# A Mamba and attention kernel on one core: mask weights on VectorE, the turned u copied by ScalarE, a first turn that waits for its own loads, 15 images a block

## The chip, the cores and the metric

The kernel runs on one core of one Trainium2 chip. The metric is the device time of one execution in microseconds; three executions of the kernel before took 8346.27 to 8347.81 us, median 8347.58. Engine names: PE is TensorE, DVE VectorE, ACT ScalarE, POOL GpSimd, SP SyncE, which issues the transfers.

## The reference, cut to what matters

For each of 32 images (128 channels, 32 by 32 pixels, so 1024 tokens) three layers follow each other. In short:

```python
# layer 0: attention over the 1024 tokens of the image
attn = softmax(Q.T @ K * scale); t = V @ attn.T + x
# layer 1: h = LN(t) through Mamba, both directions, then layer norm and a small MLP
xc, z = split(x @ in_proj); xc = silu(conv4(xc)); dt, Bm, Cm = xc @ x_proj
h[t] = exp(dt * A) * h[t-1] + dt * Bm * xc;  y = (h * Cm).sum + xc * Dp;  y = y * silu(z)
m = fwd(y) @ out_proj + bwd(y) @ out_proj;   t2 = m + mlp(LN(m))
# layer 2: the heaviest 511 of 1024 tokens get a feed-forward, scaled by their weight
weights = x @ wr;  keep = top_k(weights)[:511];  x[keep] += gelu(x[keep] @ w1) @ w2 * weights[keep]
```

The Mamba state has 16 components for each of 256 inner channels, in two directions; the work with it is the bulk of the kernel. (Each layer adds its input to its output and the input of a layer is normed where the layer asks for it.)

## The kernel before, in words

An image's Mamba layer is 64 **steps**: four quarters (two directions, two halves of 512 tokens), each with 16 state components. At step n, with two halves of 128 channels each,

- ACT (lines 848 and 860) makes `da` = exp(dt A) and half of `ub` = u times B for step n + 2,
- POOL (L1042) makes the other half of `ub` for step n + 2, and then (L1056) `g` = h times C of step n, 128 by 1024,
- PE turns `ub` of step n + 1 into PSUM (L518) and adds the turned `g` of step n - 1 to y (L522),
- DVE scans (L1160): `h` of step n from `da` and the turned `ub`,
- SP loads the row of C for step n + 4 into a ring of four tiles `c_all` (L461), once `g` has freed the tile.

Everything else is laid beside these steps. Each step has four **slots** (4n to 4n + 3), and the tables `AT_...` and `LN_...` say in which slot an engine does which piece: on DVE scan, slots 4n and 4n+1, second scan, slots 4n+2 and 4n+3; on PE and ACT in the same way; on POOL `ub`, two slots, `g`, two slots; on SP four slots, then the load of C. An engine takes its instructions in this order and waits at each for its semaphores, so a slot is a place in a queue, not a time. In slots of the same 64 steps run

- the preparation of the next quarter k + 1 (projection, convolution, silu, dt, u): among it DTMAX and U on DVE, DTKEEP on ACT (L919), UT on PE, which turns u into PSUM, and UKEEP, the copy of the turned u to `u_tok` (L1248, DVE). `u_tok` is what both makers of `ub` read, from the quarter's first step on, two steps ahead;
- the closing of quarter k (turn y, skip, gate, project);
- the attention of the next image, through the PSUM banks X: eight blocks of scores, maximum, exponential, turn, product (AT_S to AT_T1);
- the MLP and the feed-forward of the image before: MT adds the Mamba sum to `t1_old` on POOL (L1074), T1OLD moves `t1` to `t1_old` by a transfer (L472) after both MT sums; later LN, W (the router's weights), RANK on DVE (a comparison with all 1024 weights for each block), WK, which makes the mask `is_kept` (L1286), WTIMES, `w_kept` = mask times weight on POOL (L1108), HID, GELU and FFN, T3 on DVE (L1293), OUT on PE, OUTKEEP on ACT (L950) and STORE (L475), the transfer of the result, which waits for OUTKEEP.

The images are run in **blocks** (`turns`): a first turn with the attention of image 0 alone, image 0, a loop over images 1 to 30 with `JOINED` = 5 images in each block, image 31, and a last turn that finishes it. Each block ends in a barrier of all engines, and the semaphores are cleared. Inside a block an image follows the last without one. Before all this the setup block loads 38 weights on SP (L303); DVE and ACT wait for all of them, and DVE multiplies the convolution's weights together (L334). The first turn then loads x of image 0 (L480), and PE waits for it (L730).

Of the kernel before, what the change touches and what calls it, by code (L numbers as in the profile page):

```python
# [5 lines left out]
def conv_attn_mamba_mod_kernel(nc, I, out):  # L6
# [10 lines left out]
    P = 128  # L17
# [28 lines left out]
    JOINED = 5  # L46
# [4 lines left out]
    AT_YT = (4, 68, 132, 198)  # L51
    AT_SKIP = (8, 74, 137, 202)
    AT_GATE = ((6, 6), (84, 88), (136, 154), (203, 208))
    AT_CONV = ((8, 8, 8, 9), (75, 76, 79, 81), (135, 136, 137, 152), (204, 205, 205, 205))
    AT_PROJ = (17, 74, 140, 203)
    AT_PROJKEEP = (21, 80, 143, 203)
    AT_TAPS = ((25, 26, 27), (84, 87, 87), (148, 156, 158), (208, 209, 209))
    AT_XC = (24, 86, 156, 210)
    AT_Z = ((27, 27), (86, 86), (156, 157), (157, 157))
    AT_ZKEEP = (24, 86, 157, 157)  # L60
    AT_ROWS = ((28, 28), (88, 91), (158, 163), (211, 211))
    AT_ROWKEEP = (28, 95, 164, 213)
    AT_M = ((13, 13), (92, 95), (164, 164), (212, 212))
    AT_MKEEP = (19, 98, 168, 216)
    AT_B = (32, 97, 168, 215)
    AT_BKEEP = (37, 103, 172, 218)
    AT_DT = (35, 101, 170, 215)
    AT_DTCUT = (39, 106, 175, 219)
    AT_DTEXP = (38, 106, 174, 217)
    AT_DTLN = (38, 112, 177, 217)  # L70
# [8 lines left out]
    AT_XTOK = 13  # L79
    AT_Q = (11, 12)  # L80
    AT_QKEEP = 12
    AT_K = (19, 20)
    AT_KKEEP = 23
    AT_V = (24, 27)
    AT_VKEEP = 32
    AT_S = (36, 37, 48, 48, 60, 61, 81, 81, 109, 109, 118, 118, 132, 134, 154, 154)
    AT_MAX = (43, 52, 66, 87, 114, 122, 139, 163)
    AT_EXP = (39, 52, 65, 90, 113, 122, 139, 168)
    AT_PT = (43, 52, 67, 96, 114, 124, 144, 173)
    AT_PTKEEP = (42, 55, 67, 97, 115, 123, 145, 174)  # L90
    AT_RINV = (47, 55, 74, 110, 118, 133, 148, 178)
    AT_PV = (46, 47, 55, 56, 68, 70, 106, 107, 116, 116, 127, 131, 148, 148, 178, 179)
    AT_T1 = (50, 61, 83, 110, 120, 133, 153, 182)

    LN_STATS = {0: (131, 194), 1: (15, 30), 2: (211, 213)}
    LN_AGGR = {0: (154, 195), 1: (16, 44), 2: (212, 213)}
    LN_POW = {0: 192, 1: 48, 2: 211}
    LN_APPLY = {0: (197, 197), 1: (58, 67), 2: (216, 216)}
    LN_TURN = {0: 199, 1: 182, 2: 217}
    LN_KEEP = {0: 201, 1: 180, 2: 217}  # L100

    AT_MT = (24, 30)
    AT_B2 = (29, 68)
    AT_T1OLD = 38
    AT_W1 = (184, 185, 189, 189)
    AT_HID1 = (184, 190)
    AT_LEAKY = (191, 195)
    AT_W2 = (195, 195, 195, 195)
    AT_T2 = 199
    AT_BASE = (221, 222)  # L110
    AT_W = (222, 222)
    AT_WKEEP = 221
    AT_WTURN = 225
    AT_WCOL = 229
    AT_EARLIER = 223
    AT_RANK = (230, 231, 231, 232, 234, 234, 234, 239)
    AT_WK = 240
    AT_WTIMES = 237
    AT_HID = (226, 226, 229, 229, 231, 231, 232, 232)
    AT_GELU = (227, 227, 228, 228)  # L120
    AT_FFN = (233, 233, 233, 234, 239, 239, 240, 242)
    AT_T3 = (243, 247)
    AT_OUT = 246
    AT_OUTKEEP = 248
    AT_STORE = 244
# [9 lines left out]
    FIRST_T1 = tuple(FIRST + 6 + 4 * i for i in range(8))  # L135

# [5 lines left out]
    with ctx:  # L142
# [127 lines left out]
        zeroed = ctx.enter_context(nc.semaphore("zeroed"))  # L270
        setup_exp = ctx.enter_context(nc.semaphore("setup_exp"))


        with nc.Block() as block:
            loads = [
                (wq[:], I["wq"]), (wk[:], I["wk"]), (wv[:], I["wv"]),
                (bq[:], I["bq"]), (bk[:], I["bk"]),
                (bv_rows[:], I["bv"].to_broadcast([P, C])),
# [40 lines left out]
            @block.scalar  # L319
            def _(act):  # L320
                act.wait_ge(loaded, 16 * len(loads))
                act.activation(a_neg[:], a_neg[:], ACT.Exp).then_inc(setup_exp, 1)

            @block.vector
            def _(dve):
                dve.wait_ge(loaded, 16 * len(loads))

                dve.tensor_scalar(bq[:], bq[:], SCALE, None, ALU.mult)
                dve.tensor_scalar(b1_low[:], b1[:], SLOPE, None, ALU.mult)
                dve.tensor_copy(wr_cols[:], wr[:].to_broadcast([C, P]))  # L330

                for r in range(DIRS):
                    for tap in range(KCONV):
                        dve.tensor_tensor(w_conv[:, r, tap, :], w_conv[:, r, tap, :], in_cols[:, r, 0:P], ALU.mult)  # L334
                dve.wait_ge(setup_exp, 1)
                dve.tensor_scalar(a_neg[:], a_neg[:], -1.0, None, ALU.mult)
# [65 lines left out]
            (w_col_kept, 1), (w_kept_made, 1), (w_made, 1), (w_row_kept, 1), (w_turned, 1), (x_loaded, 16),  # L402
# [9 lines left out]
        def turns(first, count, last, now, nxt):  # L412
# [32 lines left out]
            with nc.Block() as block:  # L445

                def sp_turn(sp, j):
# [31 lines left out]
                    if nxt:  # L479
                        sp.dma_start(x_in[:], I["x"][image + 1]).then_inc(x_loaded, 16)  # L480
# [25 lines left out]
                def pe_turn(pe, j):  # L506
# [103 lines left out]
                    def prepare(at, k):  # L610
# [3 lines left out]
                        if at == AT_PROJ[k]:  # L614
                            if k == QUARTERS - 1:
# [6 lines left out]
                        for tap in due(AT_CONV[k], at):  # L622
                            if tap == 0 and k == QUARTERS - 1:
# [104 lines left out]
                    def attend_next(at):  # L728
                        if at == AT_XT:
                            pe.wait_ge(x_loaded, since(x_loaded, 16))  # L730
# [93 lines left out]
                def act_turn(act, j):  # L824
# [52 lines left out]
                    def prepare(at, k):  # L877
# [133 lines left out]
                    if not now:  # L1011
                        for at in range(SLOTS * ALL):
                            aside(at)
                        if nxt:
                            for n in range(LEAD):
# [9 lines left out]
                def pool_turn(pool, j):  # L1025
# [50 lines left out]
                    def aside(at):  # L1076
# [8 lines left out]
                        if last:  # L1085
# [52 lines left out]
                def dve_turn(dve, j):  # L1138
# [71 lines left out]
                    def prepare(at, k):  # L1210
# [35 lines left out]
                        if at == AT_UKEEP[k]:  # L1246
                            dve.wait_ge(u_turned, since(u_turned, prep(k, 1, 1)))
                            dve.tensor_copy(u_tok[:, side, :, :].rearrange("p b d -> p (b d)"), banks(Y)  # L1248
                                            ).then_inc(u_kept, 1)

                    def finish_last(at):
# [29 lines left out]
                        if at == AT_WK:  # L1281
# [4 lines left out]
                            dve.tensor_scalar(is_kept[:], rank[:], float(KEPT), None, ALU.is_lt).then_inc(ranked, 1)  # L1286
                        for part in due(AT_T3, at):
                            if part == 0:
                                dve.wait_ge(w_kept_made, since(w_kept_made, 1))
# [50 lines left out]
                    if not now:  # L1340
                        for at in range(SLOTS * ALL):
                            aside(at)
# [70 lines left out]
```

## Time and profile before

| what | value |
|---|---|
| runs, median (lowest to highest) | 8347.58 us (8346.27 to 8347.81) |
| the profiled execution's own time | 8358.25 us |
| its span, first to last instruction | 8356.5 us |
| first scan of image 0; last scan's end | 134.97 us; 8255.29 us |
| mean granted TensorE clock, of full speed | 0.990 |
| instructions | 152516 |

The times of the rows are microseconds from the start of the span, unless they are marked as ns. The profiled execution is a single one; the spans of its image 8, from its first scan at 2155.23 to that of image 9 at 2407.99, are read most closely below. A share of busy time says how much of the time an engine was at work, not which engine the others waited for.

### The profile page before, as it was taken

To read this page: it belongs to the slowest core of one execution; us is meant where nothing else is said; L and a number is where in the kernel's file an instruction comes from. 1 tells how busy PE (TensorE), PEld (TensorE's weight loads), DVE (VectorE), ACT (ScalarE), POOL (GpSimd) and SP (SyncE) were. 2 spreads that over 40 slices of the span, in tenths; PEclk is the share of its full clock that TensorE was granted. 3 is DMA by queue.
4 is the path that set the end of the run, shared out by engine and by line. 5 is a ranking of instruction groups with operands and counts; after the bars stand their busy time and mean duration, and the time that the engine had idled before them with its cause. 6 is when DMAs were issued, how large, how long until landed. Compare 5 with 4: busy or idle time off the path is not lost. (4 is left out here: it accounts for less than half of the span.)

```text
span 8356.5 us, 152516 instructions
## 1 busy us (share of the span) xinstructions
PE 7891.8 (94%) x53760; PEld 6159.6 (74%) x53760; DVE 7365.4 (88%) x10156; ACT 6933.8 (83%) x11874; POOL 7487.6 (90%) x7051
## 2 busy tenths in 40 slices
PE   6999999999999999999999999999999999999986
PEld 4777777777777777777777777777777777777765
DVE  4899899898999898999989999989999989999985
ACT  4888888888888888888888888888888888888874
POOL 3999999899999899999999999989999999999985
PEclk9999999999999999999999999999999999999998
DMA  1222222222222222222222222222222222222221
GB/s 49 75 68 79 75 76 73 71 72 77 75 74 74 72 73 76 74 74 69 73 78 75 74 75 72 73 75 74 74 75 72 74 75 74 74 71 72 78 71 35
DMA packets 321339, 604.11 MB, mean 72 GB/s; under 512 B 40961, under 2 KB 43714, under 8 KB 320578
## 3 DMA queue, kind: packets, MB, share of 16 engines
q1 hardware_dynamic: 320578, 594.31, 23.0%
q8 instruction: 435, 7.13, 0.4%
q14 instruction: 326, 2.67, 0.1%
HBM read 556.42 MB, written 20.97 MB: 69 GB/s over the span
## 5 line engine op out<-in xcount | busy, mean ns | idle before, releaser
L1056 POOL TENSOR_TENSOR g<-h,c_all 128x1024 f32<-128x1024 f32 x2048 | 4861.9, 2374 | 210.4 <-DVE h L1160 119.6
L848 ACT ACTIVATE da<-dt,a_neg 128x512 f32<-128x512 f32 x4096 | 2771.4, 715 | 165.4 <-DVE h L1160 158.4
L1160 DVE TENSOR_TENSOR_SCAN h<-da,ps 128x512 f32<-128x512 f32 x2048 | 2432.2, 1210 | 447.2 <-ACT da L848 215.1
L1160 DVE TENSOR_TENSOR_SCAN h<-da,h,ps 128x512 f32<-128x512 f32 x2048 | 2544.8, 1270 | 214.7 <-PE ps L518 80.4
L518 PE MATMUL ps<-ident,ub 128*128 128x128 f32 x16384 | 2373.2, 276 | 126.0 <-DVE h L1160 107.0
L518 PEld LDWEIGHTS ps<-ident,ub 128*128 128x128 f32 x16384 | 1886.0, 141 | 761.7 <-issue 466.4
L522 PE MATMUL ps<-ident,g 128*128 128x128 f32 x16384 | 2248.7, 275 | 12.8 <-POOL g L1056 9.4
L522 PEld LDWEIGHTS ps<-ident,g 128*128 128x128 f32 x16384 | 1892.0, 141 | 421.3 <-issue 391.1
L1042 POOL TENSOR_SCALAR ub<-u_tok,b_tok 128x256 f32<-128x256 f32 x4096 | 1932.8, 488 | 208.9 <-DVE u_tok L1248 190.4
L860 ACT ACTIVATE ub<-u_tok,b_tok 128x256 f32<-128x256 f32 x4096 | 1845.8, 500 | 310.0 <-PE ps L518 219.5
L515 PE MATMUL ps<-v_tok,probs_t 128*128 128x128 f32 x4096 | 543.3, 278 | 16.4 <-ACT probs_t L966 16.4
L515 PEld LDWEIGHTS ps<-v_tok,probs_t 128*128 128x128 f32 x4096 | 491.5, 192 | 34.5 <-ACT probs_t L966 30.4
L515 PE MATMUL ps<-k_all,q 128*128 128x512 f32 x1024 | 502.1, 598 | 7.5 <-DVE t L1315 3.1
L515 PE MATMUL ps<-x_pad,w_conv 128*128 128x512 f32 x1024 | 504.9, 595 | 0.2 <-DVE xc L1193 0.2
L837 ACT ACT_TABLE_LOAD x352 | 451.6, 1283 | 6.2
L972 ACT ACTIVATE probs<-ps,nmax 128x1024 f32<-128x1024 f32 x256 | 284.5, 1111 | 106.8 <-DVE nmax L1303 100.8
L1303 DVE TENSOR_REDUCE nmax<-ps 128x1 f32<-128x1024 f32 x256 | 308.7, 1206 | 40.5 <-PE ps L515 40.5
L966 ACT ACTIVATE probs_t<-ps 128x1024 f32<-128x1024 f32 x256 | 262.2, 1024 | 86.5 <-PE ps L518 84.3
L1083 POOL TENSOR_TENSOR xc<-xc,sz 128x512 f32<-128x512 f32 x256 | 326.4, 1281 | 6.2 <-DVE xc L1193 6.2
L518 PE MATMUL ps<-ident,probs 128*128 128x128 f32 x2048 | 270.7, 275 | 59.5 <-ACT probs L972 59.5
L515 PE MATMUL ps<-tile_b,f_w 128*128 128x512 f32 x512 | 261.0, 633 | 63.4 <-ACT hid L945 40.1
L1218 DVE SCALAR_TENSOR_TENSOR ps<-x_proj,w_taps,ps 128x512 f32<-128x512 f32 x384 | 283.8, 739 | 25.8 <-ACT ps L890 12.4
(125 smaller groups left out, 9152.8 us busy)
## 6 DMA issues: line engine op xcount, KB each, us to landing
c_all<-c_rows SPq DMA_DIRECT2D x2048, 256.0 KB, 3.1
x_in<-in_x SPq DMA_DIRECT2D x32, 512.0 KB, 5.6
t_old<-t SPq DMA_DIRECT2D x32, 512.0 KB, 4.4
out<-tile_b SPq DMA_DIRECT2D x32, 512.0 KB, 2.8
c_rows<-rows SPq DMA_DIRECT2D x128, 32.0 KB, 2.7
w_conv<-in_conv_rows SPq DMA_DIRECT2D x1, 512.0 KB
f_w<-in_f_w SPq DMA_DIRECT2D x2, 256.0 KB
hid<-in_in_proj SPq DMA_DIRECT2D x1, 256.0 KB
```

Source lines behind the costliest of these rows:

```text
L515: return nc.tensor.matmul(o, a, b, start=first, stop=last)
L518: return nc.tensor.transpose(o, src, ident[:])
L522: return nc.tensor.matmul(o, src, ident[:], start=first, stop=last, is_transpose=True)
L837: nc.scalar.preload_act_table_set(name)
L848: act.activation(da[:, n % 2, half, :], dt[:, slot, half, :], ACT.Exp, scale=a_neg[:, r, half, s:s + 1]).then_inc(da_made, 1)
L860: t = act.activation(ub[:, n % 2, b, :], u_tok[:, slot, b, :], ACT.Copy, scale=b_tok[:, slot, b, s:s + 1])
L972: act.activation(probs[:], banks(att(i)), ACT.Exp, bias=nmax[:, i:i + 1], accum_out=rowsum[:, i:i + 1]).then_inc(probs_made, 1)
L1042: t = pool.tensor_scalar(ub[:, n % 2, b, :], u_tok[:, slot, b, :], b_tok[:, slot, b, s:s + 1], 1.0, ALU.mult, ALU.mult)
L1056: pool.tensor_tensor(g[:, n % 2, :, :], h[:, n % 2, :, at:at + BANK], c_all[:, n % RING, :].unsqueeze(1).to_broadcast([P, NH, BANK]), ALU.mult
L1083: pool.tensor_tensor(xc[:, slot, half, :], xc[:, slot, half, :], sz[:, slot % NCH, half, :], ALU.mult).then_inc(y_gated, 1)
L1160: dve.tensor_tensor_scan(h[:, n % 2, half, at:at + BANK], da[:, n % 2, half, :], ps[:, DB + half, :], before, ALU.mult, ALU.add).then_inc( ...
L1303: dve.tensor_reduce(nmax[:, i:i + 1], banks(att(i)), AX.X, ALU.max, negate=True).then_inc(max_made, 1)
```

## The change

Four edits, and new values in nearly all the tables of slots.

1. `JOINED` goes from 5 to 15.
2. The product of mask and weights moves from POOL (slot WTIMES) to DVE, right behind the mask, as eight operations on one column each.
3. UKEEP, the copy of the turned u, moves from DVE to ACT.
4. The setup block issues seven loads first (x of image 0 among them) on a semaphore of their own; only these are waited for there. SP's wait for the other loads goes. What DVE and ACT computed in setup moves to slot 60 of the first turn, the first turn's wait for x goes, and PE and ACT wait there for `weights_made`.

```diff
-    JOINED = 5
+    JOINED = 15
...
-    AT_ROWKEEP = (28, 95, 164, 213)
+    AT_ROWKEEP = (28, 88, 170, 212)
...
-    AT_DTMAX = (47, 117, 182, 223)
-    AT_U = (51, 118, 183, 226)
-    AT_DTKEEP = (51, 116, 180, 231)
-    AT_UT = (49, 118, 183, 239)
-    AT_UKEEP = (54, 122, 186, 242)
-    AT_CSTORE = (22, 114, 171, 212)
+    AT_DTMAX = (52, 114, 179, 227)
+    AT_U = (52, 115, 179, 230)
+    AT_DTKEEP = (52, 112, 177, 230)
+    AT_UT = (53, 116, 179, 232)
+    AT_UKEEP = (55, 116, 179, 241)
+    AT_CSTORE = (27, 109, 159, 212)
...
-    AT_MT = (24, 30)
-    AT_B2 = (29, 68)
-    AT_T1OLD = 38
+    AT_MT = (17, 22)
+    AT_B2 = (20, 68)
+    AT_T1OLD = 13
...
-    AT_HID1 = (184, 190)
+    AT_HID1 = (177, 184)
...
-    AT_RANK = (230, 231, 231, 232, 234, 234, 234, 239)
-    AT_WK = 240
-    AT_WTIMES = 237
+    AT_RANK = (234, 234, 236, 239, 239, 239, 239, 242)
+    AT_WK = 245
...
-    AT_T3 = (243, 247)
-    AT_OUT = 246
-    AT_OUTKEEP = 248
-    AT_STORE = 244
+    AT_T3 = (246, 246)
+    AT_OUT = 247
+    AT_OUTKEEP = 249
+    AT_STORE = 237
...
+    SETUP = FIRST + 12
...
+            first_loads = [
+                (x_in[:], I["x"][0]), (bq[:], I["bq"]), (wq[:], I["wq"]), (bv_rows[:], I["bv"].to_broadcast([P, C])),
+                (wk[:], I["wk"]), (bk[:], I["bk"]), (wv[:], I["wv"]),
+            ]
...
+                    for dst, src in first_loads:
+                        sp.dma_start(dst, src).then_inc(first_loaded, 16)
                     for dst, src in loads:
                         sp.dma_start(dst, src).then_inc(loaded, 16)
-                sp.wait_ge(loaded, 16 * len(loads))
...
-                dve.wait_ge(loaded, 16 * len(loads))
-
+                dve.wait_ge(first_loaded, 16 * len(first_loads))
                 dve.tensor_scalar(bq[:], bq[:], SCALE, None, ALU.mult)
...
-                    if nxt:
+                    if nxt and now:
                         sp.dma_start(x_in[:], I["x"][image + 1]).then_inc(x_loaded, 16)
...
+                        if at == AT_UKEEP[k]:
+                            act.wait_ge(u_turned, since(u_turned, prep(k, 1, 1)))
+                            act.activation(u_tok[:, side, :, :].rearrange("p b d -> p (b d)"), banks(Y), ACT.Copy
+                                           ).then_inc(u_kept, 1)
...
-                            if at == AT_WTIMES:
-                                pool.wait_ge(ranked, since(ranked, 1))
-                                pool.tensor_tensor(w_kept[:], is_kept[:], w_col[:], ALU.mult).then_inc(w_kept_made, 1)
...
-                        if at == AT_UKEEP[k]:
-                            dve.wait_ge(u_turned, since(u_turned, prep(k, 1, 1)))
-                            dve.tensor_copy(u_tok[:, side, :, :].rearrange("p b d -> p (b d)"), banks(Y)
-                                            ).then_inc(u_kept, 1)
...
+                            dve.wait_ge(ranked, since(ranked, 1))
+                            for i in range(NB):
+                                dve.tensor_scalar(w_kept[:, i:i + 1], is_kept[:, i:i + 1], w_col[:, i:i + 1], None, ALU.mult
+                                                  ).then_inc(w_kept_made, 1)
...
+                            if nxt and at == SETUP:
+                                dve.wait_ge(loaded, all_loaded)
...
+                                dve.tensor_scalar(a_neg[:], a_neg[:], -1.0, None, ALU.mult).then_inc(weights_made, 1)
```

## Rows read from the trace of the kernel before

**Rows 1.** The page's first part: busy us (share of the span) and instructions.

```profile
PE 7891.8 (94%) x53760; PEld 6159.6 (74%) x53760; DVE 7365.4 (88%) x10156; ACT 6933.8 (83%) x11874; POOL 7487.6 (90%) x7051
```

**Rows 2.** Windows of images 5, 8, 14: length, PE, PEld, DVE, ACT, POOL busy, clock.

```profile
1390.46:1647.35 256.89, 245.41 (x1692) 192.08 (x1690) 229.91 (x317) 217.11 (x373) 234.79 (x223) 1.00 0.24 74
2155.23:2407.99 252.76, 244.25 (x1682) 191.04 (x1681) 229.90 (x317) 216.32 (x372) 233.87 (x221) 1.00 0.24 74
...
3678.59:3932.99 254.40, 245.73 (x1682) 192.71 (x1681) 229.83 (x317) 216.31 (x372) 233.83 (x221) 0.99 0.23 74
```

**Rows 3.** Windows, same columns: steps 0-29, 30-46, 47-56, 57-63 of image 8.

```profile
2155.23:2267.43 112.20, 108.97 (x755) 85.43 (x754) 100.00 (x118) 97.74 (x170) 111.46 (x105) 1.00 0.27 85
2267.43:2330.91 63.48, 62.77 (x444) 50.09 (x443) 56.74 (x70) 54.04 (x92) 56.01 (x51) 1.00 0.24 72
2330.91:2372.92 42.01, 40.67 (x278) 31.05 (x276) 39.76 (x61) 39.38 (x70) 41.17 (x42) 1.00 0.19 59
2372.92:2407.99 35.07, 31.84 (x211) 24.47 (x211) 33.40 (x72) 25.16 (x41) 25.23 (x25) 1.00 0.20 63
```

**Rows 4.** Waits of POOL in image 8: us in total, times, longest.

```profile
POOL w_kept L1108 <- DVE is_kept L1286: 7.6, 1, 7.6
POOL ub L1042 <- DVE u_tok L1248: 5.1, 2, 2.6
POOL g L1056 <- DVE h L1160: 2.9, 4, 1.5
```

**Rows 5.** Timeline of POOL at step 30: start, duration, [idle before].

```profile
2271.34 0.94 POOL L1042 TENSOR_SCALAR ub<-u_tok,b_tok 128x256 f32<-128x256 f32 x2 [2.55 <-DVE u_tok L1248]
```

**Rows 6.** Timeline of setup: the last of 38 weight loads, setup's work, x, PE.

```profile
17.78 1.96 SPq L303 DMA_DIRECT2D w_rows<-in_x_proj  x3
21.65 0.26 ACT L322 ACTIVATE a_neg<-a_neg 128x64 f32<-128x64 f32 x1 [19.64 <-DMA w_rows<-in_x_proj]
...
23.54 0.19 DVE L336 TENSOR_SCALAR a_neg<-a_neg 128x64 f32<-128x64 f32 x1
23.99 0.36 SPq L480 DMA_DIRECT2D x_in<-in_x  x1
...
27.61 1.97 PE L518 MATMUL ps<-ident,x_in 128*128 128x128 f32 x8 [27.61 <-DMA x_in<-in_x]
```

**Rows 7.** Timeline of DVE in the first turn's attention, where slot 60 falls.

```profile
61.67 1.22 DVE L1303 TENSOR_REDUCE nmax<-ps 128x1 f32<-128x1024 f32 x1 [2.01 <-PE ps L515]
```

**Rows 8.** Instructions by line (xcount | busy, mean ns | idle), and one timeline row.

```profile
L1248 DVE COPY u_tok<-ps 128x1024 f32<-128x1024 f32 x128 | 154.5, 1207 | 3.8 <-PE ps L518 3.7
...
L919 ACT ACTIVATE dt<-ps 128x1024 f32<-128x1024 f32 x128 | 130.3, 1018 | 58.7 <-DVE u L1245 58.7
...
L1286 DVE TENSOR_SCALAR is_kept<-rank 128x8 f32<-128x8 f32 x32 | 5.5, 172 | 1.1
...
2358.21 0.37 DVE L1185 BATCH_NORM_AGGREGATE mean_var<-stats 128x2 f32<-128x6 f32 x4
```

**Rows 9.** Timeline of image 8's end: scans of step 59, POOL's wait for the mask.

```profile
2389.14 2.45 DVE L1160 TENSOR_TENSOR_SCAN h<-da,h,ps 128x512 f32<-128x512 f32 x2 [0.23 <-ACT da L848]
...
2395.06 0.21 POOL L1108 TENSOR_TENSOR w_kept<-is_kept,w_col 128x8 f32<-128x8 f32 x1 [7.57 <-DVE is_kept L1286]
```

**Rows 10.** Timeline around the store; landings of this load, six later, and x.

```profile
2405.34 0.34 SPq L475 DMA_DIRECT2D out<-tile_b  x1
...
2405.74 0.42 SPq L461 DMA_DIRECT2D c_all<-c_rows  x1
...
2408.74 2.35 POOL L1056 TENSOR_TENSOR g<-h,c_all 128x1024 f32<-128x1024 f32 x1
...
DMA to landing us min/median/max: 4.9/4.9/4.9
...
DMA to landing us min/median/max: 3.0/3.0/3.1
...
DMA to landing us min/median/max: 5.6/5.6/5.6
```

More of the change, by code:

```diff
@@ L45, in conv_attn_mamba_mod_kernel @@
     SLOTS = 4
-    JOINED = 5
+    JOINED = 15
     DB, YA, Y, X = 0, 2, 4, 6
[L51 to L59, printed above, removed]
@@ L91, in conv_attn_mamba_mod_kernel @@
[L91 to L100, printed above, removed]
-    AT_MT = (24, 30)
@@ new lines, in conv_attn_mamba_mod_kernel @@
+    AT_ZKEEP = (21, 79, 156, 156)
+    AT_ROWS = ((27, 28), (81, 84), (160, 161), (207, 207))
+    AT_ROWKEEP = (28, 88, 170, 212)
+    AT_M = ((12, 13), (85, 91), (164, 165), (209, 209))
+    AT_MKEEP = (17, 94, 170, 215)
+    AT_B = (32, 93, 171, 215)
+    AT_BKEEP = (37, 96, 175, 219)
+    AT_DT = (33, 95, 172, 217)
+    AT_DTCUT = (39, 99, 176, 222)
+    AT_DTEXP = (42, 103, 174, 220)
+    AT_DTLN = (45, 108, 175, 220)
+    AT_DTMAX = (52, 114, 179, 227)
+    AT_U = (52, 115, 179, 230)
+    AT_DTKEEP = (52, 112, 177, 230)
@@ new lines, in conv_attn_mamba_mod_kernel @@
+    AT_UT = (53, 116, 179, 232)
+    AT_UKEEP = (55, 116, 179, 241)
+    AT_CSTORE = (27, 109, 159, 212)
+    AT_XT = 3
+    AT_XTOK = 7
+    AT_Q = (11, 11)
+    AT_QKEEP = 14
+    AT_K = (13, 13)
+    AT_KKEEP = 18
+    AT_V = (19, 21)
+    AT_VKEEP = 20
+    AT_S = (22, 22, 45, 45, 57, 58, 77, 78, 104, 105, 120, 121, 135, 135, 152, 154)
+    AT_MAX = (27, 50, 62, 83, 110, 126, 141, 161)
+    AT_EXP = (34, 50, 61, 84, 109, 124, 141, 163)
+    AT_PT = (36, 51, 63, 91, 110, 127, 143, 168)
+    AT_PTKEEP = (38, 51, 63, 95, 110, 126, 145, 173)
@@ new lines, in conv_attn_mamba_mod_kernel @@
+    AT_RINV = (45, 52, 72, 92, 114, 132, 150, 172)
+    AT_PV = (40, 41, 52, 52, 67, 68, 99, 100, 115, 115, 131, 131, 147, 147, 173, 173)
+    AT_T1 = (46, 58, 76, 105, 119, 135, 151, 178)
+    LN_STATS = {0: (167, 178), 1: (13, 23), 2: (203, 207)}
+    LN_AGGR = {0: (177, 178), 1: (38, 47), 2: (207, 207)}
+    LN_POW = {0: 178, 1: 51, 2: 208}
+    LN_APPLY = {0: (190, 191), 1: (64, 66), 2: (211, 213)}
+    LN_TURN = {0: 197, 1: 175, 2: 216}
+    LN_KEEP = {0: 199, 1: 175, 2: 216}
+    AT_MT = (17, 22)
@@ new lines, in conv_attn_mamba_mod_kernel @@
+    AT_B2 = (20, 68)
+    AT_T1OLD = 13
+    AT_W1 = (178, 178, 183, 184)
+    AT_HID1 = (177, 184)
+    AT_LEAKY = (183, 190)
+    AT_W2 = (191, 191, 195, 195)
+    AT_T2 = 198
+    AT_BASE = (223, 226)
+    AT_W = (222, 223)
+    AT_WKEEP = 226
+    AT_WTURN = 228
+    AT_WCOL = 230
+    AT_EARLIER = 227
+    AT_RANK = (234, 234, 236, 239, 239, 239, 239, 242)
+    AT_WK = 245
+    AT_HID = (229, 229, 232, 232, 233, 233, 236, 236)
+    AT_GELU = (231, 231, 232, 232)
+    AT_FFN = (239, 239, 239, 239, 240, 240, 241, 241)
@@ L316, in _ @@
                                    base=0, pattern=[[-1, P]], channel_multiplier=1)
[L319 to L322, printed above, removed]
             @block.vector
             def _(dve):
-                dve.wait_ge(loaded, 16 * len(loads))
+                dve.wait_ge(first_loaded, 16 * len(first_loads))
                 dve.tensor_scalar(bq[:], bq[:], SCALE, None, ALU.mult)
[L329 to L336, printed above, removed]
+        all_loaded = 16 * len(loads)
         x_loaded, stored = sem("x_loaded"), sem("stored")
@@ L614, in prepare @@
                         if at == AT_PROJ[k]:
+                            if not now:
+                                pe.wait_ge(weights_made, 1)
                             if k == QUARTERS - 1:
@@ L622, in prepare @@
                         for tap in due(AT_CONV[k], at):
+                            if tap == 0 and not now:
+                                pe.wait_ge(weights_made, 1)
                             if tap == 0 and k == QUARTERS - 1:
@@ L729, in attend_next @@
                         if at == AT_XT:
-                            pe.wait_ge(x_loaded, since(x_loaded, 16))
+                            if now:
+                                pe.wait_ge(x_loaded, since(x_loaded, 16))
                             if joined:
@@ L1012, in act_turn @@
                         for at in range(SLOTS * ALL):
+                            if nxt and at == SETUP:
+                                act.wait_ge(loaded, all_loaded)
+                                tables("natural_log_exp_and_others")
+                                act.activation(a_neg[:], a_neg[:], ACT.Exp).then_inc(setup_exp, 1)
                             aside(at)
                         if nxt:
+                            act.wait_ge(weights_made, 1)
                             for n in range(LEAD):
@@ L1341, in dve_turn @@
                         for at in range(SLOTS * ALL):
+                            if nxt and at == SETUP:
+                                dve.wait_ge(loaded, all_loaded)
+                                dve.tensor_scalar(b1_low[:], b1[:], SLOPE, None, ALU.mult)
+                                dve.tensor_copy(wr_cols[:], wr[:].to_broadcast([C, P]))
+                                for r in range(DIRS):
+                                    for tap in range(KCONV):
+                                        dve.tensor_tensor(w_conv[:, r, tap, :], w_conv[:, r, tap, :], in_cols[:, r, 0:P],
+                                                          ALU.mult)
+                                dve.wait_ge(setup_exp, 1)
+                                dve.tensor_scalar(a_neg[:], a_neg[:], -1.0, None, ALU.mult).then_inc(weights_made, 1)
                             aside(at)
```

53 lines of the change are left out of this document (13 added, 40 removed).

## The prediction

> **What bounds the kernel now.** I read the shares of busy time first [rows 1]: four engines stand between 83 and 94%, so none can be called the bound from the page alone. The windows of single images come next [rows 2]: an undisturbed image inside a block takes 252.76 us, and the same engines are busy 244.25 (PE), 229.90 (DVE), 216.32 (ACT) and 233.87 us (POOL) in it. Images 1 to 30 carry over nine tenths of the span, so a microsecond in each is worth 30.
>
> Then I cut this image into four stretches [rows 3]: steps 0 to 29, 30 to 46, 47 to 56 and 57 to 63. In the first POOL is busy 111.46 of 112.20 us: POOL sets the pace there, with PE close behind (108.97). In the second PE is busy 62.77 of 63.48 us and POOL 7.5 us idle; in the third POOL is full again (41.17 of 42.01); in the last DVE is busy 33.40 of 35.07 and POOL 9.8 us idle. The waits of POOL in this image name its idle time [rows 4]: 7.6 us for `is_kept`, 5.1 for `u_tok`, 2.9 for scans. The two waits for `u_tok` are those for the quarters k=1 and k=2, at POOL's steps 30 and 46, in the second stretch; the first of them stands as a row [rows 5].
>
> The sum is made against the profiled execution, 8358.25 us, which is 10.7 (0.13%) above the median of 8347.58; I take the 10.7 off at the end. What a measurement can tell from no change is about 0.2%, 17 us.
>
> **15 images a block.** Groups of five end after images 5, 10, 15, 20, 25 and 30; groups of fifteen after 15 and 30. Four borders go. Image 5, which ends on one, takes 256.89 us against 252.76 [rows 2]: 4.1 each, **-16.5 us** for four. What the first steps after a border lose besides is not in this and would add to the gain; what an image longer in the block could lose, nothing in the rows shows.
>
> **The first turn.** SP issues the weights until 19.74 us, setup computes at 21.65, and x is issued only at 23.99, though SP's wait had ended with the others' at 21.65 [rows 6]. So a block's end holds SP until DVE is done (23.73), and PE's first work, at 27.61, follows x. After the change x goes first and nobody waits for the rest, but SP still has every other load to issue before the block can end: 19.74 + 0.4 for one more issue + 0.3 for the border gives PE a start at 20.5, **-7.1 us**, and not the 20 that the loads alone would allow. If the border waited for landings it would be -5.7; if SP held nobody, -19.6. The ten setup operations of DVE (2.1 us) move into the attention of the first turn, where DVE has a gap of 2.0 us before a reduce [rows 7]: +0.2. `a_neg` on ACT hides beside them. Sum **-6.9**.
>
> **Copy of the turned u.** It costs DVE 1207 ns, four times an image; ACT copies a tile of the same shape out of PSUM in 1018 [rows 8]. So DVE loses 4.8 us of work and ACT gains 4.1; ACT is the idlest engine. That alone is worth nothing in steps 0 to 29. It counts where POOL waits for `u_tok`. For k=1 the copy moves from slot 122, behind both scans of step 30, to 116, the start of ACT's step 29, and U from 118 to 115; POOL needs it at its own step 30, so the 2.55 us go. For k=2 (slot 186 to 179) ACT is held by DTKEEP, which waits for U at DVE's slot 179, and then by HID1: I give it 1.55 of its 2.6 [rows 4]. Gain **-4.1 an image**. The lower bound is zero, since PE is 99% busy in this stretch [rows 3] and could hold the pace; the upper is all 7.5 us of POOL's idle time there. I stand nearer to the waits, as the PE time has start-up time of its waits in it.
>
> **Weights times mask.** POOL's 7.57 us wait is the longest of all [rows 9], but POOL could use only its last part: its next product needs the scan of step 59, which ends at 2391.59, 3.5 us before the wait does. And DVE is busy in all but 1.7 us of this stretch [rows 3], so POOL's freedom can hardly shorten it. I count **0**, with bounds of 1.7 less and, for DVE's added work below, 1.4 more. On DVE the product becomes eight one-column operations. Four small aggregates stand in 0.37 us [rows 8], so eight take about 0.65; one by one at the 172 ns of `is_kept` 1.4. Against that the copy of k=3 (1.2) leaves this stretch, but its U (slot 226 to 230) enters: DVE's load there stays within 0.7 us of what it was.
>
> On such small operations the Trainium skill, "VectorE: DVE Perf Modes", section "The TRN2 errata", speaks against the change: each pays a fixed cost, about 150 cycles at 0.96 GHz as measured there, and many small tiles pay it each time. By that eight would cost an estimated 1.25 us, and the sum would be 18 us higher over 30 images. The aggregates, which pass at 0.09 us apiece, do not bear it out for a row of equal operations, so 0.65 stands.
>
> **What the slots do on SP's queue.** The diff moves two stores forward, and both wait in order on SP, ahead of the `c_all` loads. The output's store goes from slot 244 to 237 (step 59), but what it waits for, OUTKEEP, is at ACT's slot 249. The loads of c for 63, 64 and 65 then queue behind it; now only that for 65 does. That one is issued at 2405.74, 0.4 after the store, and lands in 4.9 us against 3.0 for six later ones [rows 10], thus at 2410.64. POOL comes to the product 63 at 2408.74 [rows 10]. So POOL would wait 1.9 us. T1OLD goes from slot 38 to 13 (step 3) and waits for both MT sums, the second at POOL's slot 22, after the product of step 5. Load 7 waits behind it; POOL reaches product 7 after two ub and one product, 0.95+2.37+0.95 = 4.2 us; the load lands 0.45+4.9 = 5.4 after. Wait 1.2. Both fall into steps 0 to 29, where POOL is full, so nothing covers them: **+3.1 an image**. Bounds: 0, if POOL comes later than now, and 4.5, with the 5.6 us of the x load [rows 10] in place of the 4.9. CSTORE for k=2 (171 to 159, its rows at ACT's 170) also holds SP, but load 43 has a step in hand: 0.
>
> All other slots move too. Loads per engine and stretch stay within some 3 us; I count 0 and keep 2.5 us either way. Clock: image 14 shows a mean granted clock of 0.99 and 254.40 us [rows 2], 1.6 more, from stretches at 1.2 instead of 2.4 GHz; about one image in four has such a one, and I leave that as it is.
>
> **Sum.** An image: -4.1 + 3.1 = -1.0, times 30 = -30. With -16.5 and -6.9: -53. 8358.25 - 53 = 8305 for the profiled execution, less 10.7: **8294 us** (chance 0.40, for 8216 to 8315, where an image is 0.3 to 3.6 us shorter).
>
> **Rivals.**
> - *Only the ends count.* PE's full second stretch or the SP queue eats the gain and the image stays at 252.8: 8347.6 - 23 = 8324. For it: three engines near full everywhere. Chance 0.14.
> - *POOL is freed.* SP's loads come in time and POOL's wait for the mask pays too: 5 us an image, 8347.6 - 23 - 150 = 8174. For it: POOL's 18.9 us of idle time are the largest pool that the change touches; against it: DVE is full in the last stretch. Chance 0.16.
> - *The first turn gives nothing and an image loses a little* (0.1 to 0.6): 8340. The change then doesn't do what it says, since the wait for the first loads is replaced by SP's issue. Chance 0.13.
> - *Slower: SP's queue.* The store at step 59 makes the products 63 and 7 late by the 3.1 us, and PE, already full in steps 30 to 46, gives nothing back: 8347.6 + 93 - 23 = 8417. It decides from a net loss of 1.3 us an image on (30 times 1.3 is 23 + 17). For it: POOL idles 0.7 us in 112 now, so it can absorb nothing. Against it: `u_tok` waits are real. Chance 0.17.
>
> **Range.** Leaving out about a tenth on either side: an image 4.5 shorter gives 8190, 1.7 longer 8375; the bounds of copy and queue reach both. Faster by over 0.2% takes the first three cases, 0.70; within 0.2% 0.13; slower 0.17.
>
> **What would show it.** Right: POOL waits no longer for `u_tok` at step 30 and has none at `w_kept`; instead it waits about 2 us for `c_all` at an image's start and 1.2 near step 7, with issues of three `c_all` right behind the store; PE starts at 20.5; two borders in the loop's stretch. Wrong: no waits for `c_all`, a POOL with gaps elsewhere in steps 0 to 29, or an image at 255 with DVE waiting for ACT, which has the copy now.

## The result, and the profile after

The changed kernel takes a median of **8402.88 us** (8396.68 to 8405.09, 4 runs) against 8347.69 us for the kernel before on the same chip: a ratio of **1.0066**, 95% interval 1.0054 to 1.0078. It is slower by 55 us, where 53 less were forecast. The profiled execution took 8405.09 us, with a span of 8403.3 and a mean granted clock of 0.982 of full speed.

The ends did become shorter. The first scan of image 0 comes at 126.82 us (before 134.97), and image 0 takes 236.38 us for 240.88. The loss is in the loop: the median image is 255.99 us long from first scan to first scan, where an undisturbed one of before took 252.76 [rows 2]: 3.2 us more. In the mean of the 30 images, borders and all, it is 256.23 for 254.13.

The windows of image 8 after the change, to be read beside [rows 2, 3]: the whole image, its four stretches (steps 0-29, 30-46, 47-56, 57-63), then step 0 and step 1 alone. Columns: start and end, length, busy time (and instructions) of PE, PEld, DVE, ACT, POOL, granted clock, DMA share, GB/s.

```profile
2152.60:2408.56 255.96, 246.33 (x1683) 192.81 (x1682) 227.28 (x322) 219.27 (x376) 234.17 (x220) 0.99 0.24 73
2152.60:2269.31 116.71, 111.50 (x767) 88.40 (x766) 100.51 (x118) 99.80 (x172) 110.85 (x105) 0.99 0.27 86
2269.31:2333.61 64.30, 63.45 (x437) 49.59 (x436) 56.24 (x74) 55.79 (x97) 59.48 (x56) 1.00 0.23 70
2333.61:2372.28 38.67, 37.89 (x270) 29.98 (x269) 36.18 (x50) 37.46 (x70) 38.29 (x37) 1.00 0.24 70
2372.28:2408.56 36.28, 33.48 (x215) 24.83 (x214) 34.34 (x82) 26.23 (x41) 25.55 (x25) 0.95 0.15 44
2152.60:2158.25 5.65, 2.61 (x21) 1.92 (x20) 2.33 (x2) 5.20 (x9) 3.26 (x4) 0.94 0.97 274
2158.25:2165.30 7.05, 7.05 (x40) 6.04 (x41) 6.03 (x7) 2.35 (x4) 6.71 (x7) 0.81 0.27 80
```

DVE is busy 2.6 us less than before and ACT 3.0 more, the way that the copy's move asks (4.8 and 4.1 were counted, and DVE has the mask's product now). The first stretch has grown by 4.5 us, and POOL, which had 0.7 us of idle time there, now has 5.9. Steps 0 and 1 take 12.70 us; before they took 6.61. In step 1 PE is busy throughout, but at a granted clock of 0.81.

The timeline at this image's start (start, duration, engine, instruction, idle time before it). The lines are of SP's queue, POOL and PE:

```profile
2150.37 0.34 SPq L469 DMA_DIRECT2D out<-tile_b  x1
2150.76 1.69 SPq L455 DMA_DIRECT2D c_all<-c_rows  x3
2152.64 0.34 SPq L474 DMA_DIRECT2D x_in<-in_x  x1
...
2152.81 1.04 PE L516 MATMUL ps<-ident,g 128*128 128x128 f32 x8
...
2155.78 2.34 POOL L1064 TENSOR_TENSOR g<-h,c_all 128x1024 f32<-128x1024 f32 x1 [2.39 <-DVE h L1165]
...
2158.18 1.97 PE L516 MATMUL ps<-ident,g 128*128 128x128 f32 x8 [2.53 <-POOL g L1064]
```

Three loads of c stand in one bunch behind the store, as foreseen. POOL's product waits 2.39 us. The profile names a scan, but the scan that this product reads had ended at 2152.27; the load that it reads lands at 2155.65, 4.89 us after its issue and 0.13 before the product starts. PE then waits 2.53 us for the product, and its eight turns behind that wait take 1.97 us where the same eight took 1.04 us at 2152.81: the clock has fallen to the lower of its two levels, 1.2 of 2.4 GHz.

### The profile page after: what moved, and what is told of

It is laid out like the page before. It is cut to its first block and busy times, and to the rows that moved or that the text cites. A ratio compares the mean times of both kernels' runs of the same rounds, so it can differ in the third digit from the quotient of the medians.

```text
span 8403.3 us, 152633 instructions
## 1 busy us (share of the span) xinstructions
PE 7927.8 (94%) x53760; PEld 6193.3 (74%) x53760; DVE 7277.5 (87%) x10284; ACT 7023.8 (84%) x12002; POOL 7496.8 (89%) x7019
## 5 line engine op out<-in xcount | busy, mean ns | idle before, releaser
L516 PE MATMUL ps<-ident,g 128*128 128x128 f32 x16384 | 2216.0, 276 | 85.9 <-POOL g L1064 82.8
L509 PE MATMUL ps<-v_tok,probs_t 128*128 128x128 f32 x4096 | 518.4, 276 | 29.9 <-ACT probs_t L969 29.9
L509 PE MATMUL ps<-tile_b,f_w 128*128 128x512 f32 x512 | 284.8, 684 | 32.1 <-ACT hid L948 27.4
L948 ACT ACTIVATE hid<-ps,f_b 128x1024 f32<-128x1024 f32 x128 | 142.8, 1116 | 201.0 <-PE ps L509 200.6
```

The costliest lines, as they stand in the source:

```text
L509: return nc.tensor.matmul(o, a, b, start=first, stop=last)
L516: return nc.tensor.matmul(o, src, ident[:], start=first, stop=last, is_transpose=True)
```

## The experiments

The theories. **A**: the store at slot 237 holds the loads on SP's queue. **B**: other re-timed slots, those of step 44 above all, cost the time. **C**: the edits themselves cost it. **D**, formed later: the early copy of the turned u only exchanges one wait for another. Ratios are to the kernel before, run on the same chip at the same time, with 95% intervals; the groups of experiments ran on different chips, so they are compared by their ratios.

**The store put back.**

```diff
-    AT_STORE = 237
+    AT_STORE = 244
```

> The changed kernel with the store of the output back at slot 244 and nothing else. Theory A (SP's queue: the store at step 59 waits for OUTKEEP and holds the loads of c for 63, 64 and 65, so POOL comes late to an image's first products): POOL's wait of 2.4 us at step 0 goes, 2.4 to 2.9 us an image come back, 30 times, so 8403 less 72 to 87, 8316 to 8331 us, and the period of an image falls from 256.0 to 253.2 or so. Theory B (the loss is in the re-timed slots of the middle, step 44 above all, 7.8 us where it took 2.5): no change, 8395 to 8410, since what POOL gains at the start it loses at the next full engine.

Measured 8306.30 us, ratio 0.9950 (0.9936 to 0.9963). Against the changed kernel's 1.0066 that is 0.0116 of 8348 us, 97 us or **3.2 us an image**: theory A, and more than it asked for. Windows of image 8, step 0 and step 1:

```profile
2132.18:2384.63 252.45, 245.04 (x1682) 191.50 (x1681) 227.18 (x321) 219.16 (x376) 234.17 (x220) 0.99 0.25 74
2132.18:2135.41 3.23, 2.62 (x21) 1.94 (x20) 2.33 (x2) 3.20 (x6) 3.23 (x4) 1.00 0.95 200
2135.41:2141.73 6.32, 5.92 (x40) 4.69 (x41) 5.92 (x6) 4.26 (x8) 6.32 (x7) 1.00 0.46 149
```

Steps 0 and 1 take 9.55 us, 3.15 less, at full clock. They are still longer than the 6.61 before, so the rest of the change has made step 1 longer by itself.

**The move of `t1_old` put back.**

```diff
-    AT_T1OLD = 13
+    AT_T1OLD = 38
```

> The changed kernel with T1OLD back at slot 38 and nothing else. By the term of the prediction (load 7 waits 1.2 us behind the store for t1_old): 36 us less, 8367. By the trace of the changed kernel, where POOL shows no wait near step 7: no change, 8395 to 8410. Theory B expects no change either.

Measured 8401.45, ratio 1.0064 (1.0048 to 1.0079): nothing. The timeline of the changed kernel shows why:

```profile
2184.77 0.47 SPq L466 DMA_DIRECT2D t_old<-t  x1
2185.28 1.92 SPq L455 DMA_DIRECT2D c_all<-c_rows  x3
2186.36 2.38 POOL L1064 TENSOR_TENSOR g<-h,c_all 128x1024 f32<-128x1024 f32 x1 [0.70 <-PE ps L516]
...
2189.62 2.37 POOL L1064 TENSOR_TENSOR g<-h,c_all 128x1024 f32<-128x1024 f32 x1
```

The first load behind the move is issued at 2185.28 and lands at 2189.34 (4.05 us later); the product that reads it starts at 2189.62 without a wait. It is covered by 0.3 us.

**The four edits on the old slots.**

```diff
...
-    AT_UKEEP = (55, 116, 179, 241)
+    AT_UKEEP = (54, 119, 183, 242)
...
```

(All other tables as in the kernel before.)

> The changed kernel's four edits on the slots of the kernel before (only the copies of the turned u, now on ACT, come a step earlier in two quarters: 119 for 122, 183 for 186). Theory A with the prediction's other terms: the SP loss is gone and the gains stand, 8348 - 23 (ends) - up to 123 (u copies, 4.1 an image): 8200 to 8325, and under the first experiment only by what the copies bring. Theory B (the slots are the whole loss): clearly under the first experiment, 8320 or less with the first experiment at 8400. Rival C (the edits themselves cost time, the copy on ACT or the eight small products on DVE): over 8348.

Measured 8357.70, ratio 1.0013 (1.0004 to 1.0022). The image is 253.67 us long in the median of the undisturbed ones, 0.9 more than before, with the ends gained. Theory B in the form "the slots are the whole loss" falls: with the store put back, the new slots do better than the old ones. The figure of theory A with the prediction's other terms in it, 8200 to 8325, misses too. C has a point: the edits alone are no gain.

**Five images a block again.**

```diff
-    JOINED = 15
+    JOINED = 5
```

> The changed kernel with 5 images a block in place of 15. Four borders come back. By the prediction's 4.1 us each: 16.5 more, 8419. By the trace of the changed kernel, where image 15 takes 262.5 against 256.0: 6.4 each, 26 more, 8429; less what the first image behind a border gains there (2.6 to 2.9, since no store stands ahead of its loads), 3.7 each, 8418. Theory A expects that last one, 8415 to 8420; if borders cost nothing it stays at 8403.

Measured 8426.97, ratio 1.0098 (1.0083 to 1.0113): for four borders 24 us more than the changed kernel by the medians and 27 by the ratios, **6.0 to 6.7 us each**. Theory A's 8415 to 8420 misses. The image behind a border is short, as it expected (252.7 to 253.3 us), but the one behind that is long (257.5 to 258.9).

**Fifteen images a block alone** (in the kernel before, the same edit reversed).

> The kernel before with 15 images a block and nothing else. By the prediction's term, four borders at 4.1 us: 16.5 less than before, 8329. By the run of the changed kernel with 5 images a block, where four borders cost 25 us: 8320. If what a border costs hung on the changed slots alone: 8345.

Measured 8333.07, ratio 0.9969 (0.9958 to 0.9981): 26 us less. In the kernel before, image 6 shows what a border costs besides the 4.1 us of image 5 [rows 2]; its window, and that of its steps 0 and 1:

```profile
1647.35:1902.23 254.88, 245.85 (x1671) 193.90 (x1671) 230.04 (x317) 215.95 (x371) 233.00 (x219) 0.98 0.23 73
1647.35:1654.87 7.52, 6.24 (x35) 5.85 (x35) 5.82 (x6) 4.88 (x8) 6.36 (x6) 0.59 0.54 171
```

This image takes 2.1 us more than image 8. Its steps 0 and 1, at a clock of 0.59, take 0.9 of that. Image 6 is one of the longer ones: behind the five borders of the loop the first image takes 0.4 to 2.1 us more than image 8, 1.2 in the mean, and the second 0.9 in the mean. With the 4.1 that makes 6.2 a border, where this run gives 6.1 to 6.5.

**The store at 237 in the old kernel.**

```diff
-    AT_STORE = 244
+    AT_STORE = 237
```

> The kernel before with the store of the output at slot 237 in place of 244 and nothing else: the suspected cost put into the old kernel. Theory A by the prediction's term (product 63 waits 1.9 us): 57 more, 8402; by what the first experiment gave back (97 us): 8442. Theory B (it was some other slot, and the store cost only in that company): 8345, no change.

Measured 8428.43, ratio 1.0086 (1.0070 to 1.0101): 72 us, 2.4 an image, between the two figures of A; B would have had none. Windows of image 8, then its steps 0, 1 and 2:

```profile
2171.03:2426.45 255.42, 245.19 (x1683) 192.75 (x1681) 230.28 (x318) 216.25 (x372) 233.94 (x221) 0.99 0.24 74
2171.03:2176.33 5.30, 2.60 (x21) 1.92 (x20) 2.33 (x2) 4.76 (x8) 3.26 (x4) 1.00 0.86 281
2176.33:2179.90 3.57, 3.57 (x22) 3.57 (x23) 3.46 (x3) 0.79 (x2) 3.57 (x5) 0.64 0.25 83
2179.90:2183.69 3.79, 3.79 (x27) 3.31 (x26) 3.68 (x5) 2.17 (x4) 3.79 (x4) 0.89 0.25 75
```

Step 0 takes 5.30 us for 3.23, and the clock falls to 0.64 right behind it. POOL's wait there was 2.04 us, close to the 1.9 that the prediction gave the old times.

**The copy of the turned u on ACT alone, and the product of weights and mask on DVE alone** (both in the kernel before).

```diff
-                            dve.tensor_copy(u_tok[:, side, :, :].rearrange("p b d -> p (b d)"), banks(Y)
...
+                            act.activation(u_tok[:, side, :, :].rearrange("p b d -> p (b d)"), banks(Y), ACT.Copy
...
-                                pool.tensor_tensor(w_kept[:], is_kept[:], w_col[:], ALU.mult).then_inc(w_kept_made, 1)
+                                dve.tensor_scalar(w_kept[:, i:i + 1], is_kept[:, i:i + 1], w_col[:, i:i + 1], None, ALU.mult
...
```

> The kernel before with the copy of the turned u on ACT and nothing else (at slots 54, 119, 183, 242, the latest that ACT's own products leave). By the prediction's lower bound (the wait is for the copy's late place, not for its engine): 0, 8345. By its full term, 4.1 us an image, 123 less: 8222. Rival C (the edits cost time, and this is the one: POOL's waits for u_tok became 5.8 us from 5.2 with all edits on these slots): 0.9 more an image, 8372.

> The kernel before with the product of weights and mask on DVE, column by column, and nothing else. By the prediction's term: 0 to 1.4 us an image either way, 0 likeliest, 8345. If POOL's freedom pays (its wait of 7.6 us goes): up to 1.7 less an image, 8294. Rival C, the eight small operations in the stretch where DVE is full: 0.65 to 1.4 more an image, 8365 to 8387.

The copy alone: 8388.83, ratio 1.0037 (1.0023 to 1.0051), 31 us slower. The waits of POOL in its image 8 (us in total, times, longest):

```profile
POOL w_kept L1112 <- DVE is_kept L1286: 7.6, 1, 7.6
POOL ub L1046 <- ACT u_tok L922: 5.7, 2, 3.4
```

Where 5.1 us were waited for DVE's copy [rows 4], 5.7 are waited for ACT's. A faster engine (1015 ns a copy instead of 1207) does not bring `u_tok` earlier when its place in the queue is late.

The mask alone: 8371.13, ratio 1.0013 (1.0004 to 1.0022), 11 us or 0.36 us an image. POOL's wait of 7.6 us, the longest of all, was worth nothing.

**The first turn alone** (the kernel before with the setup edit).

```diff
+                    for dst, src in first_loads:
+                        sp.dma_start(dst, src).then_inc(first_loaded, 16)
...
-                sp.wait_ge(loaded, 16 * len(loads))
```

> The kernel before with the first turn's own loads ahead of the others and the setup moved into its attention, and nothing else. By the prediction's term: 6.9 less than before (ratio 0.9992). By the trace of the changed kernel, whose first scan of an image comes 8.1 us earlier: ratio 0.9990. If the first turn gives nothing: 1.0000. All three lie near what a measurement can tell, so the first scan's time in the trace decides: 134.97 before, 127 to 128 if the term holds.

Measured 8350.89, ratio 0.9993 (0.9984 to 1.0002), so not told from no change by the times. The trace has its first scan at 127.06, 7.9 us earlier, and PE's first work here:

```profile
21.02 1.94 PE L513 MATMUL ps<-ident,x_in 128*128 128x128 f32 x8 [21.02 <-PEq L278]
```

**Two variations on the kernel of the first experiment:** the mask's product back on POOL, and work taken out of step 44.

```diff
+    AT_WTIMES = 243
...
-    LN_STATS = {0: (167, 178), 1: (13, 23), 2: (203, 207)}
-    LN_AGGR = {0: (177, 178), 1: (38, 47), 2: (207, 207)}
-    LN_POW = {0: 178, 1: 51, 2: 208}
+    LN_STATS = {0: (167, 184), 1: (13, 23), 2: (203, 207)}
+    LN_AGGR = {0: (177, 184), 1: (38, 47), 2: (207, 207)}
+    LN_POW = {0: 185, 1: 51, 2: 208}
```

> The first experiment's kernel (the change with the store back at slot 244) with the product of weights and mask put back on POOL, at its slot 243. If the eight small products cost what they cost alone in the old kernel, 0.35 us an image: 11 less than the first experiment, ratio to before 0.9938 where that had 0.995. If POOL, which waits again for the mask, comes late for the product of step 61: 0.9955 to 0.9965.

> The first experiment's kernel with the second half of the statistics of the first layer norm, their aggregates and the power moved from slots 178 to 184 and 185: about 1.5 us of DVE's work leave the heap of step 44, where DVE has 5.1 us of other work between two scans and POOL waits 2.3. Theory B (this heap is a loss of its own and explains why the early copy of the turned u paid nothing): up to 1.5 us an image, 45 less, ratio to before 0.9896. Rival (the work is only moved, DVE or PE pays it two steps later): 0.995, as the first experiment.

The mask on POOL: 8301.05, ratio 0.9934 (0.9920 to 0.9947); 0.0016 better than the first experiment, with overlapping intervals. Step 44 relieved: 8334.68, ratio 0.9973 (0.9963 to 0.9984), *worse* by 0.0023 with the intervals touching, outside both expectations, so theory B's heap is not a matter of DVE's load. Why it is worse was not followed up. DVE's timeline from the second scan of step 44 to the first of step 45, here:

```profile
2310.34 1.19 DVE L1165 TENSOR_TENSOR_SCAN h<-da,ps 128x512 f32<-128x512 f32 x1
2311.45 0.33 DVE L1320 SCALAR_TENSOR_TENSOR t<-ps,rinv,x_tok 128x128 f32<-128x128 f32 x1
2312.84 1.42 DVE L1243 SCALAR_TENSOR_TENSOR ps<-ps,b_dt,dt 128x512 f32<-128x512 f32 x2 [1.06 <-ACT dt L914]
2314.29 1.22 DVE L1250 TENSOR_TENSOR u<-ps,xc 128x1024 f32<-128x1024 f32 x1
2315.43 1.21 DVE L1165 TENSOR_TENSOR_SCAN h<-da,ps 128x512 f32<-128x512 f32 x1
```

With the statistics gone DVE idles 1.06 us for ACT's logarithm of dt, and the scan starts 5.1 us after the other as it did with them (2298.73 to 2303.83 in the first experiment). On DVE the length of the step is set by the chain dt, ACT, maximum, u, which now stands whole ahead of the scan. POOL's wait in this step has another cause, a transfer on SP (see the part on why the prediction was wrong).

**The store behind all loads.**

```diff
-    AT_STORE = 237
+    AT_STORE = 249
```

> The changed kernel with the store of the output at slot 249, behind all loads of the image, and nothing else. Theory A: as the first experiment at least, 0.995; and as the load for 65 and that of x no longer queue behind the store, up to 2 us more at step 1, where 6.2 us go by and PE waits 0.4 for x: 0.988 to 0.995. If the load of x is what is late and comes later still: over 0.995.

Measured **8293.16**, ratio 0.9925 (0.9911 to 0.9938). It stands 0.0025 under the first experiment, with the intervals just touching; the step 1 of image 8 takes 5.98 us instead of 6.32.

**The chain of one quarter moved back; the copy moved back to DVE; both repairs** (each with the store at 249).

```diff
-    AT_U = (52, 115, 179, 230)
+    AT_U = (52, 115, 183, 230)
...
-    AT_UKEEP = (55, 116, 179, 241)
+    AT_UKEEP = (55, 119, 182, 241)
```

(The first pair of lines is of the first kernel, which for k=2 also has DTMAX at 182, DTKEEP at 180, UT and UKEEP at 183; the second pair is of the second kernel, which has the copy's lines on DVE as before the change. The third has WTIMES on POOL at 243.)

> The changed kernel with the store at slot 249 (as in the experiment before), and for k=2 alone the maximum of dt, u, its turn and its copy moved back by some four slots (182, 183, 183, 183), so that the scans of step 45 stand ahead of u on DVE. Theory D (the early copy only exchanges waits: what POOL no longer waits for u_tok, DVE's scan waits behind u in step 44): step 44 falls from 7.8 to under 4 us, a wait of POOL for u_tok of some 2 us comes back at step 46 or 47, and the time stays within 0.1% of 0.9925 of before. If the early copy does pay its 1.55 us for k=2: 0.998. If the heap is the loss and no wait comes back: 0.987.

> The changed kernel with the store at slot 249 and the copies of the turned u back on DVE, at slots 55, 119, 182 and 241. By the prediction (the copy's engine counts, since DVE's load and place make u_tok late): u_tok waits at steps 30 and 46 come back and an image takes up to 4.1 us more, ratio up to 1.007. By the runs of the single edits (with the copy on ACT alone an image took 0.9 us more): 0.9 less, 0.989. Theory D (waits are exchanged, either engine pays): within 0.2% of 0.9925.

> The changed kernel with the store at slot 249 and the product of weights and mask back on POOL at its slot 243: the two repairs together, as a version that may beat both kernels. By the sum of their single effects (the mask 0.0016 of the time, the store 0.0108): 0.991. If they share one wait at an image's end: 0.9925.

The chain moved back: 8318.10, ratio 0.9959 (0.9946 to 0.9973). Step 44 falls to 5.89 us, not under 4, and POOL waits 1.29 us for `u_tok` again at step 46. The time is 0.0034, 0.9 us an image, worse; theory D's "within 0.1%" misses. The early copy of k=2 does pay, but 0.9 and not the 1.55 I gave it. POOL's wait for "scans" in step 44 stays, 2.34 us where the kernel of slot 249 has 2.23, so the place of u does not make it.

The copy on DVE: 8446.28, ratio 1.0115 (1.0099 to 1.0130), 0.0190 or 5.3 us an image worse, against theory D and the single edits. In these slots the copy follows the turn so closely that DVE stands still ahead of it, and the scans behind it with DVE. Its timeline in step 13:

```profile
2481.24 1.20 DVE L1161 TENSOR_TENSOR_SCAN h<-da,ps 128x512 f32<-128x512 f32 x1
2484.41 1.22 DVE L1249 COPY u_tok<-ps 128x1024 f32<-128x1024 f32 x1 [1.97 <-PE ps L512]
2485.55 2.32 DVE L1161 TENSOR_TENSOR_SCAN h<-da,ps 128x512 f32<-128x512 f32 x2
```

So the figure holds for this place of the copy; a table made for a copy on DVE would leave room, which was not tried.

Both repairs: **8283.94**, ratio **0.9920** (0.9906 to 0.9933), the fastest of the study, faster than both kernels; it isn't told apart from the store's repair alone.

## Why the prediction was wrong

- **The main step that failed: the copy's gain of 4.1 us an image**, which was read off POOL's waits for `u_tok`, "All other slots move too" being counted at 0 and the clock left as it was. The waits did go: no `u_tok` row is left in image 8. But with the store out of the way (at 249) an image is 252.21 us long against 252.76, so copy, slots and mask together gave 0.5. The four quarters of 16 steps, image 8 of the kernel before and then of that one:

```profile
2155.23:2216.16 60.93, 59.19 (x405) 45.90 (x404) 52.93 (x70) 53.04 (x92) 60.60 (x58) 1.00 0.29 91
2216.16:2275.18 59.02, 57.11 (x406) 45.66 (x405) 54.38 (x57) 50.29 (x88) 56.06 (x53) 1.00 0.23 73
2275.18:2334.71 59.53, 58.59 (x412) 46.35 (x409) 52.95 (x64) 51.70 (x89) 54.43 (x50) 1.00 0.24 72
2334.71:2407.99 73.28, 69.35 (x464) 53.13 (x465) 69.64 (x130) 61.28 (x105) 62.78 (x63) 1.00 0.20 63
```

```profile
2133.09:2195.19 62.10, 60.58 (x411) 46.92 (x410) 54.15 (x69) 52.59 (x88) 61.06 (x59) 1.00 0.27 88
2195.19:2252.31 57.12, 55.75 (x402) 45.02 (x401) 52.18 (x56) 52.67 (x94) 55.66 (x52) 1.00 0.25 75
2252.31:2313.90 61.59, 60.66 (x417) 47.11 (x416) 53.85 (x72) 53.60 (x91) 57.04 (x55) 1.00 0.23 70
2313.90:2385.30 71.40, 68.17 (x459) 52.42 (x458) 67.08 (x128) 60.43 (x104) 60.30 (x58) 0.98 0.22 66
```

  Steps 16 to 31 gain 1.9 us, most of the 2.55 of k=1, and steps 48 to 63 gain 1.9; steps 0 to 15 lose 1.2 and steps 32 to 47 lose 2.1. POOL's idle time is 18.2 us for 18.9 (length less busy time). The waits that the profile gives to scans rose from 2.9 [rows 4] to 9.5 us. Of these, 4.3 stand in step 60, where POOL had waited 7.6 for the mask, and 2.2 before product 43 are in truth a wait for a load (next point). So theory D's exchange of waits is not shown: with the chain of k=2 moved back, the wait for `u_tok` returns and those for scans stay at 9.6. Why steps 0 to 15 lose is open.
- **CSTORE for k=2, counted 0 because "load 43 has a step in hand".** It has not. The transfer stands at slot 159, its rows come at ACT's slot 170, and load 43 is the next on SP's queue. Image 8 of the changed kernel, SP, then POOL:

```profile
2317.81 0.32 SPq L462 DMA_DIRECT2D c_rows<-rows  x1
2318.17 6.41 SPq L455 DMA_DIRECT2D c_all<-c_rows  x5
...
2321.86 2.38 POOL L1064 TENSOR_TENSOR g<-h,c_all 128x1024 f32<-128x1024 f32 x1 [2.48 <-issue]
```

  The scans of step 43 had ended at 2318.99. Load 43 is the first of the five; it lands at 2321.73, 0.13 us before the product starts. In all of the images 1 to 30 POOL waits 2.2 to 2.7 us here and starts 0.13 behind the landing; in the kernel before, load 43 lands over 9 us ahead and POOL does not wait. This is the store's mechanism a second time, in every kernel with the new slots. What it costs is not shown, since no run moved this transfer alone; the quarter in which it lies loses 2.1.
- **The clock, "I leave that as it is".** In steps 55 to 58 the granted clock falls in 8 of the images 1 to 30 of the kernel before, and in 22 with the new slots and the store at 249. Steps 57 and 58 of that kernel, image 8 and then image 9, where it does not fall:

```profile
2349.04:2358.50 9.46, 8.01 (x45) 5.24 (x44) 9.24 (x18) 8.20 (x12) 9.25 (x10) 0.82 0.16 57
2601.35:2610.79 9.44, 7.52 (x47) 5.10 (x46) 9.23 (x18) 8.19 (x12) 9.23 (x10) 1.00 0.18 54
```

  The fall does not lengthen these two steps, but step 59 behind them takes 11.41 us for 10.42. The four images without any fall inside a block (9, 10, 24 and 25) take 251.3 to 251.4 us, the 22 with this one 252.3 in the median. So where the clock held, copy, slots and mask gave 1.4 us and not 0.5. With the chain of k=2 moved back the clock falls here in 3 images only, and an undisturbed one takes 252.6: the early copy of k=2 is worth 1.3 us where the clock holds, near the 1.55, and 0.9 by the times. Why the fall comes with these slots is open.
- **Store: mechanism right, size too small.** The wait at an image's start was put at 1.9 us and measured 2.39. The clock was left out of it. In image 5 of the changed kernel it did not fall at the start, and that image is 254.92 us long; image 8, where it fell, 255.96. So the wait cost about 2.5 and the clock another 1.0, in 26 of 30 images: by times 3.2, and 3.9 against the slot behind all loads.
- **T1OLD**: 1.2 us counted (its own rows, 5.35 less 4.27, give 1.1), none measured. The load behind it landed 4.05 us after its issue and not 4.9, and POOL came 4.9 us after the sum and not 4.2.
- **Borders**: 16.5 us counted, 24 to 27 measured. What was left open as "what the first steps after a border lose" is 0.9 us in steps 0 and 1; about 2 us each are lost over the two images behind, and what the rest of that hangs on was not tried.
- **First turn**: PE starts at 21.02 (20.5 said), first scan 7.9 us earlier, by times 6 with an interval across zero; 6.9 was right within what can be told.
- **Mask**: 0 counted, 0.36 us an image measured, inside the bounds. The eight products stand in 1.06 us in the trace (0.65 said). On this the Trainium skill, "VectorE: DVE Perf Modes", section "The TRN2 errata", was nearer with its fixed cost, by which eight take an estimated 1.25.
- **The sum.** An image was to gain 1.0 us and lost 3.2. With copy and slots that give 0.5 in place of 4.1 (3.6 off) and a store at 3.2 to 3.9 in place of 1.9 (1.3 to 2.0 off), less 1.2 for T1OLD, the difference of 4.2 is made up within half a microsecond. The fourth rival, "Slower: SP's queue", had the store's mechanism, and its 8417 was nearest, in part by luck: 1.2 of its 3.1 us were for T1OLD, which cost nothing, and the clock was not in it.
- **The signs.** Most of those named for "right" were seen: no wait for `u_tok`, none at `w_kept`, three loads in a bunch and a wait of 2 us at an image's start, two borders. They show that the mechanisms were there; they do not price them. Of those named for "wrong", one was seen as well: besides the wait at the start, POOL idles 3.5 us in steps 0 to 29.

## What to carry to other kernels

A queue that waits in order makes the slot of a store part of the path of every load behind it: place a store no earlier than the work that produces it, and behind the loads that the next steps need. Check this for every store on the queue: a second one here did the same and was taken for something else. Where the profile names an engine whose work had long ended, look for the landing of a load just ahead of the start. Idle time named after one late operand is not yet a gain: what moves along with the edit, slots and clock, has to be priced too. When new slots and new edits come together, test them apart: here the edits on old slots were slower, the edits on new slots faster, and one line of the table hid it.

## What the runs showed of the hardware that was not expected

Ahead of the fall of the clock in image 8 of the changed kernel stands a wait of PE of 2.53 us, in work that is otherwise full; behind it a stretch runs at the lower of the two clock levels. In steps 0 and 1 of the images 1 to 30 the granted clock is under 1.00 in 26 images of the changed kernel, in 6 of the kernel before (image 1 and the five behind a border in the loop) and in 2 with the store at slot 249 (images 1 and 16). The old kernel with its store at 237 shows it too, 0.64 in step 1 of image 8. In image 5 of the changed kernel the same stall passed without it, so it is not bound to follow. Where it does, image 8 against image 5 puts the cost at about 1 us beyond the stall's own length. Behind the five borders in the loop of the kernel before, steps 0 and 1 take 7.5 us for 6.6, at a clock of 0.56 to 0.77.

The profile put POOL's waits for a load down to a scan, or to nothing ("issue"), at products 63 and 43 alike. There the product started 0.13 us behind the landing, and over 2.5 us behind the end of the scans that it reads.
